# The next batch's rows turned in 32 by 32 blocks on VectorE and placed by SBUF-to-SBUF transfers

## What is computed

```
xn  = layernorm(x)                                  # over the 256 columns
q, k, v = split(xn @ wqkv);  q, k = relu(q), relu(k)  # 16 heads of 16
y   = (q . cumsum(k v^T)) / (q . cumsum(k) + 1e-5)  # causal linear attention, per head
cw  = top-2 weights of sigmoid(xn @ Wr), 8 routes, scaled to sum 1
ffn = sum over e < 4 of cw[e] * (silu(xn @ Wg[e]) * (xn @ Wu[e])) @ Wd[e]
      + (cw[4] + cw[6]) * xn + cw[7] * relu(xn) + causal_conv(xn, 4 taps per column)
out = x + y @ wo + ffn
```

## Time and profile before

| | |
|---|---|
| time, median of 3 runs | 1334.67 us (1334.45 to 1334.83) |
| the profiled execution | 1334.1 us, span from first to last instruction 1332.3 us |
| PE busy | 1312.0 us, 98% of the span |
| DVE busy | 1120.6 us, 84% |
| POOL busy | 822.7 us, 62% |
| ACT busy | 737.4 us, 55% |
| mean granted clock of PE | 0.997 of full |

### The profile page before, as it was taken

How to read it: one execution, slowest core, us unless ns; L and a number is a source line. 1 busy time by engine, 2 the same in 40 slices (tenths; PEclk the granted TensorE clock), 3 DMA queues, 4 the chain that set the end, 5 groups by cost and what they waited for, 6 DMA issues and landing times.

```text
span 1332.3 us, 54753 instructions
## 1 busy us (share of the span) xinstructions
PE 1312.0 (98%) x24384; PEld 1136.9 (85%) x24384; DVE 1120.6 (84%) x2574; ACT 737.4 (55%) x1543; POOL 822.7 (62%) x673
## 2 busy tenths in 40 slices
PE   5999999999999999999999999999999999999998
PEld 4888888888888888888888888888888888888887
DVE  7988889888898888898888988888888889888885
ACT  5645566545556455565555564556645655545561
POOL 2676566675575755666656757556666566575554
PEclk9999999999999999999999999999999999999999
DMA  5011211111211111111111011111111111111110
GB/s 181 30 39 66 66 53 47 35 66 66 66 34 50 51 66 65 50 50 35 66 66 65 35 49 51 66 66 50 50 34 67 66 65 35 35 65 50 51 49 18
DMA packets 46828, 73.73 MB, mean 55 GB/s; under 512 B 6529, under 2 KB 42241, under 8 KB 42497
## 3 DMA queue, kind: packets, MB, share of 16 engines
q1 hardware_dynamic: 45888, 69.23, 15.2%
q10 hardware_dynamic: 704, 1.01, 0.2%
HBM read 53.18 MB, written 17.04 MB: 53 GB/s over the span
## 4 chain that ended last, share of the span: by engine, by line
PE 97%; DVE 1%; POOL 0%; ACT 0%; DMA 0%; issue 0%; POOLq 0%; DVEq 0%
PE ring L303 51%; PE scores L303 17%; PE ring L423 7%; PE ring L439 6%; PE scores L372 5%; PE state_sum L386 4%; PE ring L459 2%; PE scores L312 2%; PE scores L354 2%; DMA x_t<-in_L_attn_x_dram 0%; DVE cT L828 0%; ACT qp L548 0%; DVE sm L807 0%; PE scores L321 0%; POOL hid L687 0%
## 5 line engine op out<-in xcount | busy, mean ns | idle before, releaser
L687 POOL TENSOR_TENSOR hid<-hid,cwb 128x512 f32<-128x512 f32 x128 | 172.0, 1343 | 225.4 <-DVE hid L836 224.7
L828 DVE SCALAR_TENSOR_TENSOR cT<-xT,conv_ws,cT 128x512 f32<-128x512 f32 x192 | 292.3, 1561 | 0.0
L675 POOL TENSOR_TENSOR x_t<-x_t,same 128x1024 f32<-128x1024 f32 x32 | 76.9, 2404 | 242.7 <-ACT same L557 242.7
L814 DVE TENSOR_TENSOR state_bd<-state_sum,tables_s 128x256 f32<-128x256 f32 x248 | 103.7, 418 | 135.9 <-PE state_sum L386 135.8
L578 ACT ACTIVATE sg<-ring 128x512 f32<-128x512 f32 x128 | 76.8, 600 | 251.3 <-PE ring L303 251.3
L303 PE MATMUL ring<-xl,wgu_h 128*128 128x512 f32 x512 | 212.3, 415 | 0.0
L691 POOL TENSOR_TENSOR hl<-hid,hh 128x512 fp32r<-128x512 f32 x128 | 208.4, 1628 | 0.0
L303 PE MATMUL ring<-xh,wgu_l 128*128 128x512 f32 x512 | 203.0, 396 | 0.0
L303 PE MATMUL ring<-xh,wgu_h 128*128 128x512 f32 x512 | 202.2, 395 | 0.0
L511 ACT ACTIVATE yh<-yT 128x256 fp32r<-128x256 f32 x128 | 53.5, 418 | 246.5 <-DVE yT L845 246.5
L807 DVE TENSOR_TENSOR sm<-scores,causal_s 128x512 f32<-128x512 f32 x256 | 158.5, 679 | 21.6 <-PE scores L372 21.6
(11 more groups left out here) (118 smaller groups left out, 3528.1 us busy)
## 6 DMA issues: line engine op xcount, KB each, us to landing
cwb<-cw_rows SPq DMA_DIRECT2D x32, 1024.0 KB, 4.7
x_t<-in_L_attn_x_dram SPq DMA_DIRECT2D x32, 512.0 KB, 4.4
out_dram<-x_t SPq DMA_DIRECT2D x31, 512.0 KB, 2.9
cw_rows<-cwt SPq DMA_DIRECT2D x128, 2.0 KB, 1.4
sm<-in_L_attn_wqkv_dram ACTq DMA_DIRECT2D x2, 384.0 KB, 5.0
sm<-in_L_ffn_Wg_dram SPq DMA_DIRECT2D x2, 256.0 KB, 3.5
sm<-in_L_ffn_Wu_dram SPq DMA_DIRECT2D x2, 256.0 KB, 4.6
cwb<-in_L_ffn_Wd_dram SPq DMA_DIRECT2D x1, 512.0 KB, 5.7
```

The costliest lines, as they stand in the source:

```text
L675: pool.tensor_tensor(xb, xb, same[:, :, :], ALU.add).then_inc(s_base1, 1)
L687: pool.tensor_tensor(hid[:, e, :], hid[:, e, :], cwb[:, e, :], ALU.mult).then_inc(s_hid, 1)
L814: dve.tensor_tensor(state_bd[:, n % 4, :].rearrange("p (g m n) -> p g m n", g=C, m=PPG), ST.unsqueeze(2).to_broadcast([P, C, PPG, BLK]), s ...
L828: ins = dve.scalar_tensor_tensor(out=cT[:, c, :], in0=xT[:, j % 2, c, n:n + BT], scalar=conv_ws[:, c, n:n + 1], in1=cT[:, c, :], op0=ALU.m ...
```

## The change

PE no longer transposes the next batch's rows, except for batch 0's own rows at the start. Instead DVE turns xn in blocks of 32 by 32 (`turn_x`): four instructions of 128x256, which write into `xb_t`, a view of `qks_tok`. A block turned in place still lies on the partitions of its source rows. So SP moves the blocks to where they belong: `place_turned` issues 32 transfers from SBUF to SBUF for each batch, 16 for each half c of the columns, each from 32 partitions to 32 partitions, four pieces of 128 bytes per partition. `xT` now has 32 columns ahead of the batch's own (LEAD), the last three of which hold the convolution's halo; it lies at another place in SBUF.

DVE turns the rows at the start of the batch, ahead of the first blocks; in batch 0 it does so after attend(0). SP places them behind the store of the batch before, ahead of the wait for that store and of the next load. ACT's `fill_xT` becomes `lead`, which copies the halo only; `high_x` waits for the transfers (`xT_in[c]`, one semaphore for each half).

```diff
+        xb_t = qks_tok.rearrange("p c n -> p (c n)").rearrange("p (c q t n) -> p c q t n", c=C, q=QUADS, t=T)
...
+        def turned_at(s, j, k):
+            return (s * BPS + j + k) * (16 * QUADS * QUADS)
...
+            def place_turned(s, j, k):
+                sp.wait_ge(s_turn, at(s, j, 1, k))
+                for c in range(C):
+                    for a in range(QUADS):
+                        for q in range(QUADS):
+                            row = xT[q * BLK:(q + 1) * BLK, (j + k) % 2, c, LEAD:LEAD + BT]
+                            sp.dma_start(row.rearrange("p (t a n) -> p t a n", t=T, a=QUADS)[:, :, a, :],
+                                         xb_t[a * BLK:(a + 1) * BLK, c, q, :, :]).then_inc(xT_in[c], 16)
...
                     sp.wait_ge(s_out, at(s, j, T, 2 * T))
                     sp.dma_start(out_v[b], x_t[:, j]).then_inc(stored, 16)
+                    if left > 1:
+                        place_turned(s, j, 2)
                     sp.wait_ge(stored, at(s, j, 16, 16))
...
             spread_cw(0, 0, 0)
+            place_turned(0, 0, 1)
             rounds(batch)
...
-            def turn_xn(s, j, k, c):
-                pe.wait_ge(s_xn, at(s, j, 1, k + 1))
-                pe.wait_ge(s_sm, at(s, j, U * ROWS, U * ROWS))
-                for t in range(T):
-                    ins = nc.tensor.transpose(XB[c][:, t * P:(t + 1) * P], xn[:, (j + k) % 2, t, c * P:(c + 1) * P],
-                                              ident_s[:, :])
-                ins.then_inc(s_xtr, 1)
...
             def heads(s, j, k):
                 p = (j + k) % 2
+                if k:
+                    pe.wait_ge(s_sm, at(s, j, U * ROWS, U * ROWS))
                 pe.wait_ge(s_xh, at(s, j, C, k * C + C))
...
-                    if t == 1 and not last:
-                        for c in range(C):
-                            turn_xn(s, j, 1, c)
...
-                for c in range(C):
-                    act.wait_ge(s_xtr, at(s, j, C, k * C + c + 1))
-                    copy(xT[:, p, c, HALO:HALO + BT], XB[c][:, :]).then_inc(s_xT, 1)
...
                 for c in range(C):
-                    act.wait_ge(s_xT, at(s, j, C, k * C + c + 1))
-                    copy(xh[:, p, c, :], xT[:, p, c, HALO:HALO + BT]).then_inc(s_xh, 1)
+                    act.wait_ge(xT_in[c], turned_at(s, j, k))
+                    copy(xh[:, p, c, :], xT[:, p, c, LEAD:LEAD + BT]).then_inc(s_xh, 1)
...
+            def turn_x(s, j, k):
+                dve.wait_ge(s_xn, at(s, j, 1, k + 1))
+                for t in range(T):
+                    ins = dve.transpose(xb_t[:, :, :, t, :], xn[:, (j + k) % 2, t, :]
+                                        .rearrange("p (c q n) -> p c q n", c=C, q=QUADS))
+                ins.then_inc(s_turn, 1)
...
+                if not last and s + j:
+                    turn_x(s, j, 1)
                 for t in range(T):
                     if t < T - 1:
                         blocks(s, j, 0, 2 * t + 2)
...
                     attend(t)
+                    if s == j == t == 0:
+                        turn_x(0, 0, 1)
```

More of the change, by code:

```diff
@@ L28, in layer_kernel @@
     HALO = TAPS - 1
+    LEAD = 32
+    QUADS = P // 32
     EPS_LN, EPS_DEN, EPS_W = 1e-5, 1e-5, 1e-9
@@ L83, in layer_kernel @@
         rstd = sb("rstd", [P, T])
-        xT = sb("xT", [P, 2, C, HALO + BT])
+        xT_gap = sb("xT_gap", [P, 12])
         xh, xl = sb("xh", [P, 2, C, BT], F32R), sb("xl", [P, 2, C, BT], F32R)
@@ L121, in layer_kernel @@
         cT = sb("cT", [P, C, BT])
+        xT_room = sb("xT_room", [P, 8])
+        xT = sb("xT", [P, 2, C, LEAD + BT])
+        xb_t = qks_tok.rearrange("p c n -> p (c n)").rearrange("p (c q t n) -> p c q t n", c=C, q=QUADS, t=T)
         rdT = qks
@@ L174, in layer_kernel @@
         s_xT = sem("s_xT")
+        s_turn = sem("s_turn")
+        xT_in = [sem(f"xT_in{c}") for c in range(C)]
         s_xh = sem("s_xh")
@@ L516, in high_weights, with lead @@
                     copy(hi, src).then_inc(w_hi, 1)
-            def fill_xT(s, j, k):
+            def lead(s, j, k):
                 p = (j + k) % 2
                 if (j + k) % BPS:
-                    act.activation(xT[:, p, :, 0:HALO], xT[:, 1 - p, :, BT:BT + HALO], ACT.Copy).then_inc(s_halo, 1)
+                    act.activation(xT[:, p, :, LEAD - HALO:LEAD], xT[:, 1 - p, :, LEAD + BT - HALO:LEAD + BT],
+                                   ACT.Copy).then_inc(s_halo, 1)
                 else:
-                    act.activation(xT[:, p, :, 0:HALO], zeros[:, 0:C * HALO].rearrange("p (c h) -> p c h", c=C),
+                    act.activation(xT[:, p, :, LEAD - HALO:LEAD], zeros[:, 0:C * HALO].rearrange("p (c h) -> p c h", c=C),
                                    ACT.Copy).then_inc(s_halo, 1)
-                for c in range(C):
-                    act.wait_ge(s_xtr, at(s, j, C, k * C + c + 1))
-                    copy(xT[:, p, c, HALO:HALO + BT], XB[c][:, :]).then_inc(s_xT, 1)
             def high_x(s, j, k):
@@ L592, in first_tap @@
                     for c in range(C):
-                        ins = act.activation(cT[:, c, :], xT[:, j % 2, c, 0:BT], ACT.Identity, bias=conv_bs[:, c:c + 1],
+                        ins = act.activation(cT[:, c, :], xT[:, j % 2, c, LEAD - HALO:LEAD - HALO + BT], ACT.Identity, bias=conv_bs[:, c:c + 1],
                                              scale=conv_ws[:, c, 0:1])
@@ L607, in batch @@
                 if not last:
-                    fill_xT(s, j, 1)
+                    lead(s, j, 1)
                 silu(2)
@@ L630, in _ @@
             act.activation(sg[:, 0:1], zeros[:, 0:1], ACT.Sigmoid)
-            act.activation(xT[:, 0, :, 0:HALO], zeros[:, 0:C * HALO].rearrange("p (c h) -> p c h", c=C),
+            act.activation(xT[:, 0, :, LEAD - HALO:LEAD], zeros[:, 0:C * HALO].rearrange("p (c h) -> p c h", c=C),
                            ACT.Copy).then_inc(s_halo, 1)
@@ L667, in low_x @@
                 pool.wait_ge(s_xh, at(s, j, C, k * C + c + 1))
-                pool.tensor_tensor(xl[:, p, c, :], xT[:, p, c, HALO:HALO + BT], xh[:, p, c, :].bitcast(F32),
+                pool.tensor_tensor(xl[:, p, c, :], xT[:, p, c, LEAD:LEAD + BT], xh[:, p, c, :].bitcast(F32),
                                    ALU.subtract).then_inc(s_xl, 1)
@@ L827, in tap @@
                     for c in range(C):
-                        ins = dve.scalar_tensor_tensor(out=cT[:, c, :], in0=xT[:, j % 2, c, n:n + BT],
+                        ins = dve.scalar_tensor_tensor(out=cT[:, c, :], in0=xT[:, j % 2, c, LEAD - HALO + n:LEAD - HALO + n + BT],
                                                        scalar=conv_ws[:, c, n:n + 1], in1=cT[:, c, :],
@@ L903, in _ @@
                     dve.wait_ge(s_xh, 1)
-                ins = dve.tensor_scalar(xT[:, 0, c, HALO:HALO + BT], XB[c][:, :], 1.0, None, ALU.mult)
+                ins = dve.tensor_scalar(xT[:, 0, c, LEAD:LEAD + BT], XB[c][:, :], 1.0, None, ALU.mult)
                 ins.then_inc(s_xT, 1)
@@ L908, in _ @@
                 dve.wait_ge(s_xh, c + 1)
-                dve.tensor_tensor(xl[:, 0, c, :], xT[:, 0, c, HALO:HALO + BT], xh[:, 0, c, :].bitcast(F32),
+                dve.tensor_tensor(xl[:, 0, c, :], xT[:, 0, c, LEAD:LEAD + BT], xh[:, 0, c, :].bitcast(F32),
                                   ALU.subtract).then_inc(s_xl, 1)
```

## The result

The changed kernel takes 1713.63 us, median of 4 runs (1710.89 to 1720.01), beside 1334.70 for the kernel before: 1.2846 times as long, 95% interval 1.2819 to 1.2874. The profiled execution took 1712.16 us, its span is 1710.4. I had forecast 1413, at most 1500: slower was right, the size was not.

A forecast was written before the change was run, and what follows sets the result against it. TensorE alone was taken to bound the kernel. A 3.3 us stall at numerators(3) less 0.85 saved, +2.45 a batch for 30 batches, and +5.4 in batch 0, added 79 to 1334.1: 1413 us, range 1318 to 1500.

The forecast's parts named there:

- The bound, and what a wait costs: On the chain that ended last: TensorE's own work holds 97%, so a wait put before TensorE costs its full length.
- TensorE's turns, 0.85 us a batch: In TensorE's stream: removing the eight transposes of turn_xn saves 0.85 us for each of 31 turns, at most 26 us.
- Rival B: On the SP queue, chance 0.12: the transfers are hidden and the full 0.85 x 31 is saved, 1308 us.
- VectorE's turns, hidden from TensorE: On VectorE at the batch's start: four block turns take 1.6 us within 2.60 us of idle time, costing nothing there.
- The 32 transfers: On the SP queue: issues 0.46 us apart, as for cw_rows, so the last starts 14.2 us after the first.
- My upper bound of 0.78: On the SP queue: at most 0.78 us per issue, 24 us in all, as three 512 KB loads at the start.
- Packets: On the DMA engines: 10 ns per 128-byte packet, so 0.09 us a transfer against 0.46 of issue.
- C: On the DMA engines, chance 0.09: 128-byte packets at 70 ns bind the transfers, +8.45 us a batch, about 1600 us.
- Landing 1.4: On the transfers into xT: the data land 1.4 us after the issue.
- Landing to numerators(3), 2.0 us, and silu(3) behind xh: On ScalarE after the data land: xh, hh, yh and silu(3) in program order take 2.0 us before numerators(3) starts.
- The tail's lag of 1.35: On VectorE: its tail ends 1.35 us later in the batch, so the turns start at 2.04 and SP issues from 3.70.
- Behind numerators(3): On TensorE: xl arrives about when silu(3) does and heads needs it 1.54 us later, so no further stall.

## Why the prediction was right or wrong

- **The bound, and what a wait costs.** Right: a wait put before TensorE cost its full length.
- **TensorE's turns, 0.85 us a batch.** Right as a place in the stream, wrong as a gain. The 26 us assumed that the rest of the stream stays as it is; without transfers the change gives nothing (1336.7), and about 14 of it with the instruction count kept (1320.83). Rival B's 1308 was not reached at any issue spacing tried, nor without the transfers: the gaps in the score products stood in its way.
- **VectorE's turns, hidden from TensorE.** Right: 1.42 us, and 0.65 of idle time left behind them.
- **The 32 transfers, the step that failed.** The term was 30 x 0.46 + 0.37 = 14.2 us between the first and the last start; measured in the batch at 828.66 it is 853.16 - 831.33 = 21.83. 20.0 of that is the spacing, 0.645, and 1.86 three long issues. I took the row nearest in size, whose far end is DRAM, and carried it to transfers with SBUF at both ends. The runs into and out of DRAM show the 0.47 again, and with it trains of 18.4, where I had 14.2 and one issue. The other half of the step is that I took four issues of one batch for the whole row, and so put the long issues at nothing, though the trace of before has them. My upper bound of 0.78 held the value, but my range did not: 24 us would have given some 1700, and I closed the range at a spacing of 0.55.
- **Packets.** Right: 11.4 ns each; C falls.
- **Landing 1.4.** 1.85 to the start of xh here.
- **Landing to numerators(3), 2.0 us, and silu(3) behind xh.** Right: 2.00, the place and the chain of the waits as told.
- **The tail's lag of 1.35.** Wrong, and small: the first issue is 2.67 after the gate product, where I had 3.70 with the lag and 2.85 without: the turn waited for GpSimd's xn, as it would have before, and not for VectorE's tail. With sixteen transfers, whose train is nearer to the one forecast, the tail does end last and the first issue is 3.04 after.
- **Behind numerators(3).** I let the batch go on as before. The slow clock after the stall adds 1.5 us.

The terms close. Against the forecast batch of 43.08 us (40.63 + 2.45): first issue -1.03, train +7.66 (21.83 for 14.17), landing +0.44, landing to numerators(3) -0.03, behind it +1.54 (23.32 for 21.78): +8.58, and 51.67 is 8.59 more. Over 30 batches of 52.7 us on average, the one above having a short train, this is 30 x 9.6 = 289 of the 299 us by which the profiled run missed 1413; batch 0 makes the rest, 58.7 us for 42.5 + 5.4. Of the 9.6 a batch, 5.8 are the spacing, 2.6 the long issues and 1.2 all the rest.

That the issue train is nearly the whole of it can be read from the runs too: trains of 23.19 and 18.44 us give 1713.6 and 1569.5, 0.98 us of time for each us of train. Drawn on to my 14.2 + 0.4 it is 1569.5 - 31 x 0.98 x 3.8 = 1454, an estimate, 41 us above 1413; the terms beside the train, of which the slow clock is the largest, make 0.9 a batch or 28 of them. With a train of 12.7 the line would give 1395, where sixteen transfers took 1423, so it holds for long trains alone. The mechanism was right; the size of one term was off, and for two reasons.

Open stays why a start costs 0.17 more with SBUF at both ends, and by what path a fetch of TensorE's instructions holds up an issue on SP. That the two go together is seen in every run with a train, and in the run with 85 more TensorE instructions a batch both counts rose by 21; no run took the fetches away.

## What to carry to other kernels

A transfer's price has three parts, its start on the issuing queue, its packets and its landing; where 32 small ones stand in a row, the start alone counts, so cut their number first (16 of twice the size took 12.7 us in place of 23.2). Take a start's price only from a row with the same kind of memory at both ends, and over all its issues, not those of one batch, so that the long ones are counted; where there is no such row, let the range go to the upper bound. And a stream of TensorE from which instructions are taken can lose the gain in gaps of its own: look whether the "issue" waits grow.

## What the runs showed that I had not expected

- Starts on SP: 0.645 us apart from SBUF to SBUF, 0.47 with DRAM at either end, whatever the pieces (128 or 512 bytes: 0.645 and 0.63) and the size (16 or 32 KB: 0.645 and 0.655). Three or four starts in a train of 32 take 0.8 to 2.0 us, each beside a 16 KB packet of instructions: 100 packets and 100 long starts in 30 trains, 122 and 121 with TensorE given 85 more instructions a batch.
- TensorE stood 0.9 to 1.8 us inside a run of 64 small products in 11 of 31 batches once 8 turns a batch were gone, each time until 1.3 to 1.5 us after such a packet, and no longer with 8 tiny ones put back: 1336.7 and 1320.83 us.
- Keeping TensorE's clock up over a 10 us stall (0.982 for 0.892) gave no more than 5 us of 1713.
